# Norms of twelve tile pairs in rounds on ScalarE and GpSimd, four and three adjacency units in turn, and search trials with two dependent operations

## What is computed

```python
R = S + eye(N); R = R / R.sum(-1)              # S is adj
for n in range(2):
    A = top_p_attention(Xa, W1, W2, W3)        # softmax of (Xa W1' W2')(Xa W3')', the smallest
                                               # probabilities dropped beyond a mass of 0.9
    Xf = R @ Xf
    Xa = A @ Xa
    Z = Z + Xf @ U1[n].T + Xa @ U2[n].T
h = X + Z
y = (h - mean(h)) / sqrt(var(h) + 1e-5) * ln_g + ln_b
out = layernorm(x + y)                         # without gain and bias
```

## Time and profile before

| | |
|---|---|
| median of 3 runs | 1553.54 us (1553.44 to 1553.98) |
| profiled execution | 1554.54 us, its span 1552.8 us |
| TensorE (PE) busy | 1222.1 us, 79% |
| VectorE (DVE) busy | 1386.8 us, 89% |
| ScalarE (ACT) busy | 893.1 us, 58% |
| GpSimd (POOL) busy | 197.2 us, 13% |
| chain that ended last | PE 46%, DVE 39%, ACT 7% |

### The profile page before, as it was taken

How to read it: one execution, slowest core, us unless ns; L and a number is a source line. 1 busy time by engine, 2 the same in 40 slices (tenths; PEclk the granted TensorE clock), 3 DMA queues, 4 the chain that set the end, 5 groups by cost and what they waited for, 6 DMA issues and landing times.

```text
span 1552.8 us, 29309 instructions
## 1 busy us (share of the span) xinstructions
PE 1222.1 (79%) x9162; PEld 1035.3 (67%) x9162; DVE 1386.8 (89%) x7148; ACT 893.1 (58%) x1737; POOL 197.2 (13%) x357
## 2 busy tenths in 40 slices
PE   8889999999989988979797949367844819276970
PEld 3767777777768968778787848366744718265970
DVE  4779999999859899889898989999998989899984
ACT  4688887887765566565555535334642525335435
POOL 0300000000103414142312010000000101000000
PEclk9999999999999989899899979779887959688985
DMA  5100000000023505041313221203030301203101
GB/s 188 46 2 1 2 2 2 2 2 2 23 112 102 190 20 177 26 153 46 133 45 133 89 89 46 89 1 133 21 113 2 133 0 51 84 1 133 46 1 44
DMA packets 16589, 96.41 MB, mean 62 GB/s; under 512 B 1251, under 2 KB 8930, under 8 KB 9730
## 3 DMA queue, kind: packets, MB, share of 16 engines
q1 hardware_dynamic: 16384, 94.14, 17.4%
HBM read 92.43 MB, written 1.70 MB: 61 GB/s over the span
## 4 chain that ended last, share of the span: by engine, by line
PE 46%; DVE 39%; ACT 7%; issue 5%; DVEq 1%; POOL 0%; DMA 0%; SPq 0%; ACTq 0%; POOLq 0%
PE bank L551 24%; PE bank L530 10%; DVE junkC L799 10%; DVE cand L748 9%; PE bank L491 8%; DVE E L1122 4%; ACT E L625 3%; DVE E L1124 2%; PE bank L566 2%; DVE sub L952 1%; DVE slots L851 1%; ACT blkT L650 1%; DVE junkS L799 1%; ACT H L714 1%; DVE st L808 1%
## 5 line engine op out<-in xcount | busy, mean ns | idle before, releaser
L650 ACT ACTIVATE blkT<-bank 128x512 f32<-128x512 f32 (+1 forms) x728 | 411.9, 566 | 445.9 <-PE bank L530 441.1
L748 DVE MAX8 cand<-E 128x8 f32<-128x32 f32 (+1 forms) x2992 | 391.0, 190 | 12.3 <-ACT E L602 11.7
L551 PEld LDWEIGHTS bank<-X,blkT 128*128 128x128 f32 x2704 | 330.5, 192 | 102.1 <-ACT blkT L650 64.9
L551 PE MATMUL bank<-X,blkT 128*128 128x128 f32 (+1 forms) x2704 | 376.0, 282 | 13.1 <-ACT blkT L650 10.5
L530 PE MATMUL bank<-ident,E 128*128 128x128 f32 x1144 | 187.9, 291 | 220.7 <-DVE E L1124 220.7
L530 PEld LDWEIGHTS bank<-ident,E 128*128 128x128 f32 x1144 | 147.5, 152 | 223.8 <-DVE E L1124 222.4
L799 DVE SCALAR_TENSOR_TENSOR junkC<-cand,st 128x128 f32<-128x128 f32 (+1 forms) x416 | 285.0, 722 | 4.2
L530 PE MATMUL bank<-ident,S 128*128 128x128 f32 x1560 | 240.3, 274 | 1.8 <-POOL S L412 1.8
L491 PE MATMUL bank<-kT,Q 64*128 64x512 f32 (+1 forms) x728 | 197.2, 615 | 7.5 <-ACT E L602 6.9
L551 PE MATMUL bank<-YA,blkT 128*128 128x128 f32 x1352 | 190.0, 285 | 8.4 <-ACT blkT L650 8.4
L602 ACT ACTIVATE E<-bank 128x512 f32<-128x512 f32 (+1 forms) x308 | 158.2, 567 | 63.5 <-PE bank L491 62.6
(11 more groups left out here) (200 smaller groups left out, 1139.5 us busy)
## 6 DMA issues: line engine op xcount, KB each, us to landing
S<-in_adj_dram SPq DMA_DIRECT2D x50, 1663.5 KB, 7.0
S<-in_adj_dram SPq DMA_DIRECT2D x2, 1455.6 KB, 8.6
X<-in_x_dram SPq DMA_DIRECT2D x6, 256.0 KB, 5.1
out_dram<-H SPq DMA_DIRECT2D x2, 768.0 KB
S<-in_adj_dram SPq DMA_DIRECT2D x2, 194.9 KB, 9.2
u_in<-in_L_gnn_U_dram SPq DMA_DIRECT2D x4, 64.0 KB, 10.4
w_in<-in_L_gnn_W_dram SPq DMA_DIRECT2D x2, 32.0 KB, 2.2
X<-in_x_dram SPq DMA_DIRECT2D x1, 64.0 KB
```

Of the source, the lines that this page charges most:

```text
L551: m = pe.matmul(bank[int(u.acc)][:, 0:width], blkT[:, slot, b * P:(b + 1) * P], rhs[:, j, 0:width], start=(j == 0), stop=(j == NT - 1))
L650: act.activation(blkT[:, slot, 0:w], BLK[early][slot][:, 0:w], ACT.Copy).then_inc(blk_done, 1)
L748: v.max(cand[:, par, xx, 8 * r:8 * r + 8], E[where_e[self.s, self.p]][:, xx, r * w:min((r + 1) * w, N)]).then_inc(s_max, 1)
```

## The change

There are six parts.

- `STEP_R` is 4 and 3 in turn for ten bodies, then 3, 3, 0. The sum is the same; bodies 1 and 3 have one unit less, bodies 6 and 8 one more.
- In step two the exponentials of bodies with four R units stand at six consecutive steps from step 36 on, one piece each. In bodies with three they all stand at step 36, the body's end, as before.
- In step two the exponential of the candidates is two activations for each tile, on the first five and the last three of each run's eight, with sums of their own (`csum`, `csum_low`). The first two coarse trials go over the first five alone (520 columns), then `csum_low` is added to the budget.
- A trial has two dependent operations instead of three; the product with the next factor (`NEXT`) is posted between the two passes. At the head of the search one `link` becomes a `post`.
- The norms of pairs 0 to 11 are cut into six rounds a pair. In each, ScalarE does one activation for each tile (sum, sum of squares, scaling, and the same again), then GpSimd its operations of 1, 7, 3, 1, 7 and 0. ScalarE runs the jobs of a unit behind the third chunk's multiplication, GpSimd behind the unit's addition; `norm_rounds` gives each pair one round a unit, from the unit after its last part on. Rounds that would come after the last R unit stand at the start of body 12, on ScalarE ahead of its block copies, with a Sqrt on one column behind them that loads the table.
- The last two tiles are finished by VectorE, which reads their PSUM banks itself and applies gain and bias; ScalarE only takes two square roots for each. The output goes out in four writes: 22 tiles, two, one, one.

```diff
-    STEP_R = [4] * 5 + [3] * 7 + [0]
+    STEP_R = [4, 3] * 5 + [3, 3, 0]
...
-            b.exps[(2 + STEP_R[p]) * NCH + 1] = [(1, p + 2, k) for k in range(6)]
+            for k in range(6):
+                b.exps.setdefault(5 * NCH + 1 + (k if STEP_R[p] > 3 else 0), []).append((1, p + 2, k))
...
+    ROUNDS = 6
+    norm_rounds = {}
+    ended = {u.pair: u for u in units if not u.turned}
+    last_part = units[-3]
+    for u in sorted((ended[p] for p in range(NPAIR - 1)), key=lambda u: u.k):
+        for r in range(ROUNDS):
+            norm_rounds.setdefault(min(u.k + 1 + r, last_part.k + 1), []).append((u.pair, r))
+    norm_at = {}
+    for k in sorted(norm_rounds):
+        norm_rounds[k].sort(key=lambda job: (job[1] if k > last_part.k else 0))
+        for job in norm_rounds[k]:
+            norm_at[job] = len(norm_at)
...
+            def norm_round(p, r):
+                t = slice(2 * p, 2 * p + 2)
+                n = norm_at[p, r]
+                pool.wait_ge(act_round, 2 * n + 2)
+                if r % 3 == 0:
+                    pool.tensor_scalar(mv[:, t], mv[:, t], -1.0 / D, None, ALU.mult).then_inc(pool_round, 1)
+                elif r % 3 == 1:
+                    then(pool.tensor_scalar(sd[:, t], sd[:, t], 1.0 / D, LN_EPS, ALU.mult, ALU.add))
+                    then(pool.tensor_tensor(rs[:, t], sd[:, t], minus_half[:, :], ALU.pow))
+                    then(pool.tensor_tensor(newton[:, :], rs[:, t], rs[:, t], ALU.mult))
+                    then(pool.tensor_tensor(newton[:, :], newton[:, :], sd[:, t], ALU.mult))
+                    then(pool.tensor_scalar(newton[:, :], newton[:, :], -0.5, 1.5, ALU.mult, ALU.add))
+                    then(pool.tensor_tensor(rs[:, t], rs[:, t], newton[:, :], ALU.mult))
+                    pool.tensor_tensor(shift[:, t], mv[:, t], rs[:, t], ALU.mult).then_inc(pool_round, 1)
+                elif r == 2:
+                    pool.wait_ge(g_loaded, 32)
+                    h = H[:, t, :]
+                    then(pool.tensor_tensor(h, h, gb[:, 0:1, :].to_broadcast([P, 2, D]), ALU.mult))
+                    then(pool.tensor_tensor(h, h, gb[:, 1:2, :].to_broadcast([P, 2, D]), ALU.add))
+                    pool.tensor_tensor(h, h, X0[:, t, 0:D], ALU.add).then_inc(pool_round, 1)
...
                 if u.turned:
                     save(u)
-                else:
+                elif u.k <= last_part.k:
                     add_part(u)
+                    for job in norm_rounds.get(u.k + 1, ()):
+                        norm_round(*job)
...
-                act.activation(cand[:, par, xx, 0:NC[s]], cand[:, par, xx, 0:NC[s]], ACT.Exp,
-                               bias=negm[:, par, xx:xx + 1], scale=1.0, accum_out=csum[:, par, xx:xx + 1])
+                pieces = [(0, 8, csum)] if s == 0 else [(0, RANKS, csum), (RANKS, 8, csum_low)]
+                for lo, hi, total in pieces:
+                    c = cand[:, par, xx, 0:NC[s]].rearrange("p (n k) -> p n k", k=8)[:, :, lo:hi]
+                    act.activation(c, c, ACT.Exp, bias=negm[:, par, xx:xx + 1], scale=1.0,
+                                   accum_out=total[:, par, xx:xx + 1])
...
+            def norm_round(p, r):
+                if r == 0:
+                    act.wait_ge(h_taken, ended[p].m + 1)
+                else:
+                    act.wait_ge(pool_round, pool_rounds(norm_at[p, r - 1]))
+                act.wait_ge(act_round, 2 * norm_at[p, r])
+                for t in (2 * p, 2 * p + 1):
+                    h = H[:, t, :]
+                    if r % 3 == 0:
+                        ins = act.activation(junkA[:, t % 2, :], h, ACT.Identity, accum_out=mv[:, t:t + 1])
+                    elif r % 3 == 1:
+                        ins = act.activation(junkA[:, t % 2, :], h, ACT.Square, bias=mv[:, t:t + 1], accum_out=sd[:, t:t + 1])
+                    else:
+                        ins = act.activation(h, h, ACT.Identity, bias=shift[:, t:t + 1], scale=rs[:, t:t + 1])
+                    ins.then_inc(act_round, 1)
...
+                if b.p == NPAIR - 1 and b.s:
+                    for job in norm_rounds.get(last_part.k + 1, ()):
+                        norm_round(*job)
+                    act.wait_ge(act_round, 2 * len(norm_at))
+                    act.activation(junkA[:, 0, 0:1], ones[:, 0:1], ACT.Sqrt)
...
+                    if 0 <= m < len(b.seqs) and seq_chunk[b.seqs[m]] == 2 and seq_unit[b.seqs[m]].k <= last_part.k:
+                        for job in norm_rounds.get(seq_unit[b.seqs[m]].k, ()):
+                            norm_round(*job)
...
                     link.post(below(scratch(0), c(0), one(THR, 0), one(LOW, 0)))
+                    link.post(v.tensor_scalar(two(NEXT), two(THR), n, None, ALU.mult))
                     link(below(scratch(1), c(1), one(THR, 1), one(LOW, 1)))
                     link(v.tensor_tensor(two(PICK), two(LOW), two(BUDGET), ALU.is_le))
-                    link(v.tensor_scalar(two(PICK), two(PICK), n - n / f, n / f, ALU.mult, ALU.add))
-                    link(v.tensor_tensor(two(THR), two(THR), two(PICK), ALU.mult))
+                    link(v.scalar_tensor_tensor(out=two(THR), in0=two(PICK), scalar=1.0 / f, in1=two(NEXT),
+                                                op0=ALU.max, op1=ALU.mult))
...
+                if s:
+                    trials(link, leading, leading_scratch, FACT[0:FIRST], FACT[FIRST])
+                    link.post(v.tensor_tensor(two(BUDGET), two(BUDGET), csum_low[:, par, :], ALU.add))
+                trials(link, c, scratch, FACT[FIRST if s else 0:C], FACT[C] if F else 1.0)
...
+            dve.wait_ge(h_taken, h_parts)
+            for xx in range(2):
+                t = NT - 2 + xx
+                u = units[-2 + xx]
+                h = H[:, t, :]
+                dve.wait_ge(blk_used, u.end)
+                link(v.scalar_tensor_tensor(out=h, in0=bank[int(u.acc)][:, 0:D], scalar=a_inv[:, (STEPS * NPAIR - 1) % 2, xx:xx + 1],
+                                            in1=h, op0=ALU.mult, op1=ALU.add))
+                statistics(xx)
+                dve.wait_ge(sd_ready, 2 * xx + 1)
+                link(v.reciprocal(rs[:, t:t + 1], sd[:, t:t + 1]))
+                link(v.scalar_tensor_tensor(out=h, in0=h, scalar=mv[:, t:t + 1], in1=gb[:, 0, :], op0=ALU.subtract, op1=ALU.mult))
+                link(v.scalar_tensor_tensor(out=h, in0=h, scalar=rs[:, t:t + 1], in1=x_end[:, xx, :], op0=ALU.mult, op1=ALU.add))
+                statistics(xx)
+                dve.wait_ge(sd_ready, 2 * xx + 2)
+                link(v.reciprocal(rs[:, t:t + 1], sd[:, t:t + 1]))
+                v.tensor_scalar(h, h, mv[:, t:t + 1], rs[:, t:t + 1], ALU.subtract, ALU.mult).then_inc(out_ready, 1)
```

126 lines of the change are left out of this document (50 added, 76 removed).

## The result

The changed kernel takes 1512.53 us (median of 4 runs, 1509.09 to 1513.83); the kernel before takes 1553.49 in the same series. The ratio is 0.9734, 95% interval 0.9722 to 0.9746: 41 us are gone, 44 were forecast.

A forecast was written before the change was run, and what follows sets the result against it. TensorE was taken to bound the kernel until about 838 us, then VectorE, then a VectorE-ScalarE tail. Terms 1.1 - 20.3 - 1.4 - 2.55 - 20.8 = -44.0 took the span from 1552.8 to 1508.8: 1509 us, range 1493 to 1526.

The forecast's parts named there:

- (1): Rival: norms weigh little, GpSimd costs VectorE 4 us and left-over rounds 3, not 9: 1493 us; chance 0.13.
- (2): Rival: TensorE or ScalarE becomes the bound, 2 us in each of eight bodies: 1525 us; chance 0.10.
- (3): Rival: strided passes are as dear as full ones, 12 x 1.3 us back: 1525 us; chance 0.08.
- (4): Rival: each GpSimd operation takes its whole length from VectorE, 65 us more: 1574 us; chance 0.03.
- Search, -2.2 us: Each step-two search: shorter trials -0.85, 520-column passes -1.30, search start -0.12, added budget operation +0.07; bounds -0.9 and -2.4.
- more tiles go the costly way: Step-two searches: cruder first trials might add fallbacks at 22 us a tile; forecast took no change, the same six tiles.
- Four bodies, -20.3: 551 to 845.35 us: exponentials spread and units alternated, VectorE takes over from TensorE, 4 x 68.5 = 274.0 us.
- Seven searches, -1.4: 845.35 to 1446.10 us: shorter searches to 585.3, GpSimd interference +12 (4 to 25), body 6 +2, giving 599.3 us.
- Last search, -2.55: Last pair's search before the tail: 2.2 us as in other searches plus 0.35 from its fine trials; 47.5 before.
- Step one, 0 (-2 to +2): 46 to 551 us, with setting up step two: TensorE is full, so shorter searches gain nothing; maxima come 1 us later.
- start of step two, +1.1: Before the second search: split candidate exponentials cost ScalarE 0.56 us a pair, two pairs on the path; bounds 0 to 2.
- Tail, -20.8: After the last pair's first tile is handed over: 38.4 us instead of 59.2, left-over rounds costing 9 (3 to 13).

The follow-up runs named there:

- no_norms: Changed kernel with the norms of the first twelve pairs left out, on ScalarE too: 1492.8 us, ratio to before 0.9607.
- old_units: Changed kernel with the old spread of adjacency units, four in each of the first five bodies, then three: 1506.6 us, ratio to before 0.9696.
- full_passes: Changed kernel with all seven coarse trials of step two at 832 candidates and candidate exponentials in one piece a tile: 1519.7 us, ratio to before 0.9783.
- three_op: Changed kernel with trials of three dependent operations as before, in both steps: 1514.1 us, ratio to before 0.9742.
- no_wide: Changed kernel with GpSimd's three 256-column operations of round 2 replaced by one short memset: 1495.5 us, ratio to before 0.9624.
- maxima_early: Changed kernel with one maximum of the next pair issued behind the added operation of each coarse trial in step one: 1509.18 us, ratio to before 0.9707.
- no_leftover: Changed kernel without the four left-over rounds of pair 11 (its rounds 2 to 5): 1504.3 us, ratio to before 0.9680.
- tail_spread: Changed kernel with pair 11's left-over rounds 3 to 5 and the Sqrt table load set behind block copies of the last body: 1503.6 us, ratio to before 0.9674.
- hidden: Changed kernel with maxima_early, tail_spread and GpSimd's 256-column operations of pairs 0 to 9 and 11 held back to run under MATCH_REPLACE8: 1493.83 us, ratio to before 0.9606.

## Why the forecast was right, and where it wasn't

**The total** came out within 0.3% (1509 against 1512.5), faster as forecast, but no term was exact: they are off by 1.2 to 3.6 us, with both signs. That the sum is closer than its terms is luck: the seven searches and the tail came out 6.4 us better than forecast, the four other terms 6.1 worse, and the time up to the first search, which was no term, 1.3 shorter. Of the rivals, (1) fell with no_norms, 9.3 us shorter in the seven searches where it had 4, (2) with old_units and no_norms as far as the bodies go (step one did lose time to a ring through ScalarE), (3) with the passes, (4) with the seven searches.

**Search, -2.2 us.** Right in the pieces: a trial 2.73 to 2.60, the 520-column pass 0.755. The rivals "strided passes are as dear" and "more tiles go the costly way" are gone: the same six tiles fell back. full_passes and three_op give 1.0 and 0.75 for the two halves in the seven searches, 1.75 together, where the pieces say 2.1. Against the kernel before, the seven searches of no_norms are 14.2 us shorter, 2.0 each.

**Four bodies, -20.3: measured -18.4.** Right in the mechanism. VectorE took over, with waits for exponentials gone after the first body, as its waits between 553 and 826 us show, beside the 11.6 us of the earlier trace rows:

```profile
DVE st L906 <- ACT E L679: 1.9, 1, 1.9
```

Periods are 70.4, 69.0, 68.5, 68.1 where 68.5 was forecast. The 2 us are mostly the first. The forecast of a six-unit body with the exponentials spread, 69.0, fits old_units, where four of them take 69.1 on the mean. Of the two parts meant for this stage the spread alone would have done.

**Seven searches, -1.4: measured -5.0.** The shorter search was to give 15.4 and gives 14.2 (no_norms). The price of GpSimd was forecast at 12 and is 9.3 in no_norms, 10.6 in no_wide, with the split wrong: all of it on the wide ones, none on the short. The 2 us for body 6 did not come: searches 20 and 24, without fallback, take 69.4 each, interference included. The Trainium skill, SBUF — State Buffer, "Who interferes with whom", says that a VectorE instruction with two SBUF inputs and a GpSimd instruction that reads SBUF exclude each other, and that the one that comes second blocks fully. The trace agrees in both directions: GpSimd's 0.19 us operation became 3.50 behind a pass of 3.69, and VectorE's two-input operation of 0.16 us (line 877, 1085.43) became 0.56 under GpSimd's 1.20 and ended with it. What kept the change from being dear (rival 4) is where VectorE spends its time: MAX8 and MATCH_REPLACE8 aren't touched (means of 189 and 1009 ns, 190 and 1008 before), and a VectorE pass that comes first makes GpSimd wait, which costs nobody anything outside the tail.

**Last search, -2.55: measured -1.1.** The forecast gave this stage no interference. no_wide has it at 44.5, 3.0 below before: the wide operations of pairs 10 and 11 fall there and take 1.8.

**Step one, 0 (-2 to +2): measured +1.5, and start of step two, +1.1: measured +2.3.** The +1.5 lies within the stated bounds, but hides more: the period from pair 2 on is 0.31 longer, ten times, and one shorter early period makes up for half of it. What the forecast passed over is that a full TensorE keeps a gain from showing, not a loss. The note that the maxima come 1 us later was right; that this closes a ring through ScalarE longer than TensorE's 28.56 was not drawn from it. At the start of step two the same late maxima cost 1.1, which maxima_early takes back; full_passes, without the split exponentials, is 1.6 shorter there, where the split was put at 1.1.

**Tail, -20.8: measured -23.6.** The mechanism is right and the term of the left-over rounds was mis-sized for this execution: 9 forecast (3 to 13), 4.6 measured, 9.9 in maxima_early. The forecast took both passes as met and the rounds as begun 3 us before the hand-over; this execution met one pass and began 7.5 before (1464.18). maxima_early met both. The rest, 26.6 - 9 = 17.6 for the last copy's end without them, is 18.3 in no_leftover; the two tiles behind it took 8.1 against 7.8, the last write 4.7 against 4 (issued 1502.59, span 1507.3). The table load took 1.28 us here with the next activation right behind (1483.25 to 1484.54 in tail_spread), as the forecast had it.

**Norms in all.** no_norms lies 19.7 us under the changed kernel: 9.3 in the seven searches, 1.9 in the last, 4.6 in the profiled tail, 1.5 in the stages ahead (no more than two traces differ by), and 2.4 that no trace shows. hidden gets within 1.0 of no_norms with all norms done, but it also has maxima_early's gain, 3.4 us in traces, which no_norms lacks.

## What to carry to other kernels

Before work is given to GpSimd beside a busy VectorE, sort both engines' instructions by who holds up whom. Here what lay under MAX8 or MATCH_REPLACE8 cost nothing, and a 256-column operation cost about half its length on the mean of 30, some under MAX8 and some beside two-input and two-column ones. A semaphore that holds such work back to the right moment gave back 7.3 of 10.6 us with all of the work still done. When a link is taken out of a dependent chain, look at what rode on it: a full engine can be overtaken by a ring through other engines, here by 1%. Left-over work ahead of the last stage went for nothing between its copies, and cost 1.7 to 9.9 us before them (the tails of three_op and maxima_early less 31.0). And where two parts of a change aim at the same wait, test each without the other: here one of them (the alternation) added nothing.

## What was not expected of the hardware

- The price of 30 operations of 0.7 us on GpSimd (21 us of work undisturbed, 26.9 in the trace) was 9 to 10.6 us of VectorE, while 161 short ones of 0.2 to 0.7 us cost nothing that can be seen.
- A two-column GpSimd operation of 0.19 us takes 3.50 or 3.58 when it starts just after a 3328-column pass of VectorE, and whether a dependent chain meets one pass or two moves the whole tail by 5.3 us for the same tail of a program (35.6 and 40.9). Six traces of it range from 32.7 to 40.9.
- VectorE's `tensor_scalar` with one input was stretched too (0.69 for 0.16, under GpSimd's 256-column operation), not only the instructions with two inputs.
